# Four attention layers on one core: the order in which TensorE takes the four heads of a block of keys

## The chip, the cores and the metric

The kernel runs on one core of a Trainium2 chip. The metric is the device time of one execution in microseconds (us). Before the change three runs took 3563.54, 3566.97 and 3571.05 us; the median is 3566.97. One further execution was profiled: it took 3571.17 us, and the span from its first to its last instruction is 3569.3 us.

## The reference

Four decoder layers follow one another on x of shape (4, 512, 256), with one context ctx of the same shape; D = 256, 16 heads of 16 (the last layer: 8 heads of 32). Cut to what matters:

```python
def _L0_xattn_ref(x, context, ...):           # causal self, then cross attention, both with a length rule
    z = _mha(x, x, Wq1, Wk1, Wv1, mask0, causal=True)
    x1 = _layernorm(x + z, ln1_g, ln1_b)
    z = _mha(x1, context, Wq2, Wk2, Wv2, mask1, causal=False)
    x2 = _layernorm(x1 + z, ln2_g, ln2_b)
    z = (relu(x2 @ fc1_w.T + fc1_b) * mask0 @ fc2_w.T + fc2_b) * mask0
    return _layernorm(x2 + z, ln3_g, ln3_b)

# L1: two attentions with an integer mask each, wo, rms norms, then a mixture of 8 experts (+1 shared)
    scores = einsum('bhqd,bhkd->bhqk', q, k) / sqrt(DK)
    scores = where(mask[:, None, :, :] == 0, NEG, scores)
    attn = softmax(scores, axis=-1)
    out = einsum('bhqk,bhkd->bhqd', attn, v)     # then reshape and @ wo

# L2: two attentions with a mask, biases, wo and a layer norm, then relu(x @ w1 + b1) @ w2 + b2
# L3: one causal attention with 8 heads of 32, and a layer norm
x = L0(x, ctx); x = L1(x, ctx, mask_ik0, mask_if1); x = L2(x, ctx, mask_ik0, mask_if1); x = L3(x, ctx, ctx)
```

## The kernel before

The program runs ten stages in the order a0 a1 f0 a2 a3 moe a4 a5 f2 a6. The f and moe stages are the dense layers and have code of their own (`feed_block`). The a stages are the seven attentions: a0 is L0's causal self attention, a1 L0's cross attention, a2 and a3 are L1's two, a4 and a5 L2's two (these four have a mask), a6 is L3's. Pairs of them (a0 a1, a2 a3, a4 a5) and a6 alone are built by `attention_block`.

**Units, turns, blocks, steps.** A unit is one stage for one batch row: 16 heads, 512 queries, 512 keys. It is worked in four turns (index j, or u inside the unit) of four heads each (two heads in a6). A turn goes over four blocks of 128 keys. In a0 to a5 a block has two steps (couples = 2), each for a couple of heads; so a turn has 8 steps (halves = 8) and a unit has 16 blocks. In a6 a block has one step.

**What a step holds.** The letters in brackets are those of the list of work.

- [ST] key scores, L720: two products, keys on the partitions, of 64 rows each (a head's parts stacked; the two heads of a couple lie in partitions 0 to 63 and 64 to 127), into one of two PSUM buffers `scores`.
- [S] query scores of the turn two ahead, L753: two products of the same shape the other way round, each into one bank of a ring of three banks (RB). DVE reads each (L993 with a mask, L991 without) for the least value of each query, and so frees the bank. In the causal stages two products with the causal triangle (L759) are added.
- [exp] on TensorE the mask products, L738 (L736 the causal triangle): two products of 128 rows onto the key scores; in a1 there are none. On ScalarE the exponential of the buffer, L882, into probT.
- [PV] once a block, L774: value product of the block before (four heads, in passes of 128 rows and 32 columns), summed over the four blocks in one bank `outputs`.

The two `scores` buffers let key scores run up to two steps ahead of the exponentials; the wait is `c_exp` two steps back.

**Small and long work beside the steps.** `timetable` puts each of the other operations at a step of the unit: per turn oT (ScalarE copies `outputs`) and m (TensorE transposes the least values; ScalarE and DVE make mrow of them) at its step 1, mrows and stack (SP's transfers into Q and K) at step 2; q, k, V, mT (the mask transposed), x, c, len (a0 and a1) of the next unit, and on, ot, y, ln of the unit before (steps 2 to 7 of its first turn). All that TensorE writes in these (m, q, k, V, mT, x, c, len, on, ot, y) takes a bank of the same ring of three as S. A bank is given out in the order of the list and may be written when the third entry before has been read (`bank_free`).

**What sets the order.** `schedule` yields one list for all engines. Each engine's program walks this list and does what is its own in each entry, in order; semaphores tie them. So a change in the order of the list moves ScalarE's and DVE's work along with TensorE's. SP and POOL take only their own entries (stack, mrows, loads, norms). Before the change the list has, for every step: ST, S, exp, then the small work of that step, and at every even step the PV of the block before.

**Stacking.** `stack` (L557, L559, L565) sends 13 transfers, 15 in a0 and a1, which lay out Q and K of the turn three ahead; the first S of that turn waits for them. `minimum_rows` (L576) sends mrow into Q and is issued by SP just ahead of `stack`; it waits for m.

Of the kernel before, what the change touches and what calls it, by code (L numbers as in the profile page):

```python
# [14 lines left out]
B, S, D = 4, 512, 256  # L15
P = 128
KB = D // P
QT = S // P
# [117 lines left out]
def timetable(a):  # L136

    h, out = a.halves, []
    step = h // 4
    for qt in range(QT):  # L140
        out += [(2 + qt, "on", -1, qt), (3 + qt, "ot", -1, qt), (4 + qt, "y", -1, qt),
                (qt + (5 if a.wo else 3), "ln", -1, qt)]
    for u in range(QT):
        out += [(u * h + 1, "oT", 0, u - 1), (u * h + 1, "m", 0, u + 1),
                (u * h + step, "mrows", 0, u + 1), (u * h + step, "stack", 0, u + 3)]
    out += [(6, "len", 1, 0), (h + 6, "len", 1, 1), (6, "maskld", 1, 0), (10, "maskcv", 1, 0)]
    out += [(h + 1, "q", 1, 1), (h + 2 * step, "k", 1, 1), (2 * h + 1, "V", 1, 0), (2 * h + 2 * step, "V", 1, 1)]
    out += [(2 * h + n * step, "mT", 1, n) for n in range(QT)]
    out += [(2 * h, "cnld", 2, 0), (2 * h, "tokens", 2, 0), (2 * h + 2 * step, "norms", 2, 0),
            (2 * h + 3 * step, "kvld", 2, 0), (3 * h, "x", 2, 0), (3 * h, "x", 2, 1)]  # L150
    out += [(3 * h + step, "c", 2, 0), (3 * h + step, "c", 2, 1), (3 * h + 2 * step, "q", 2, 0),
            (3 * h + 3 * step, "k", 2, 0)]
    out += [(0, "wload", 0, 0), (1, "wscale", 0, 0), (2 * h + 3, "rawload", 0, 0)]
    return out


def wanted(work, a, st, b, first):

    n = int(st[1:])
    return {"ot": a.wo, "y": a.wo, "ln": a.ln, "len": a.length, "maskld": a.mask is not None,  # L160
            "maskcv": a.mask is not None, "mT": a.mask is not None, "cnld": a.kv == "mctx",
            "c": a.kv == "mctx", "kvld": a.kv == "ctx", "tokens": a.rms or a.length, "norms": a.rms,
            "wload": b == 1 and 1 <= n < len(ATT) - 1, "wscale": b == 2 and n < len(ATT) - 1,
            "rawload": b == 2 and first and st != "a6"}.get(work, True)


def schedule(stages, base):

    units = [(st, b) for st in stages for b in range(B)]
    end = base + len(units)  # L170
    halves = ATT[int(stages[0][1:])].halves
    couples = halves // QT
    for j in range(4 * base - 6, 4 * end + 2):
        m, u = divmod(j, 4)

        def there(g):
            return base <= g // 4 < end

        beside = {}
        for t, work, ahead, n in timetable(ATT[int(stages[0][1:])]):  # L180
            beside.setdefault(t, []).append((work, ahead, n))
        for h in range(halves):
            if there(j):
                yield ("ST", j, h)
            if there(j + 2):
                yield ("S", j + 2, h)
            if there(j):
                yield ("exp", j, h)
            for work, ahead, n in beside.get(u * halves + h, []):
                if work in ("oT", "stack", "m", "mrows"):  # L190
                    if there(4 * m + n):
                        yield (work, 4 * m + n, 0)
                    continue
                k = m + ahead
                if base <= k < end:
                    st, b = units[k - base]
                    if wanted(work, ATT[int(st[1:])], st, b, st == stages[0]):
                        yield (work, k, n)
            kb = h // couples - 1
            if h % couples == 0:  # L200
                if kb >= 0 and there(j):
                    yield ("PV", j, kb)
                if kb < 0 and there(j - 1):
                    yield ("PV", j - 1, QT - 1)

# [4 lines left out]
def build(nc, io, ctx):  # L212
# [189 lines left out]
    def attention_block(mem, stages):  # L402
# [40 lines left out]
        block = mem.enter_context(nc.Block())  # L443

        work = list(schedule(stages, base))


# [1050 lines left out]
```

How the kernel before makes its waits and increments, by code:

```python
    def wait_x(eng, st, b):  # L347
        before = ORDER[ORDER.index(st) - 1]
        if st == "a0":
            eng.wait_ge(*((c_x0, 16) if type(b) is int and b == 0 else (c_x, 16)))
        elif before == "moe":
            eng.wait_ge(c_hD.sem, c_hD.at(st, 0, 0))
        elif before[0] == "f":
            eng.wait_ge(c_xout.sem, c_xout.at(before, b, QT))
        else:
            eng.wait_ge(*x_done[before, b, QT - 1])
# [1 line left out]
    def wait_weights(eng, n):  # L359
        eng.wait_ge(c_w[n % 2], 48 * (n // 2 + 1))
# [1 line left out]
    def deviation(pool, st, b, qt, eps):  # L362
        r = qt % 2
        pool.wait_ge(c_var.sem, c_var.at(st, b, qt + 1))
        pool.tensor_tensor(ve[:, r, :], mv[:, r, 1:2], eps_of[eps], ALU.add)
        pool.drain()
        pool.tensor_tensor(rstd[:, r, :], ve[:, r, :], minus_half[:, 0:1], ALU.pow).then_inc(c_rstd.sem, 1)
# [1 line left out]
    def gain(pool, st, b, qt, gamma, beta):  # L370
        pool.wait_ge(c_xh.sem, c_xh.at(st, b, qt + 1))
        pool.tensor_tensor(xh[:, qt % 2, :], xh[:, qt % 2, :], gamma, ALU.mult)
        pool.drain()
        pool.tensor_tensor(tile(b, qt), xh[:, qt % 2, :], beta, ALU.add).then_inc(c_xout.sem, 1)
# [9 lines left out]
    def centre(dve, st, b, qt):  # L385
        r = qt % 2
        dve.wait_ge(c_rstd.sem, c_rstd.at(st, b, qt + 1))
        dve.wait_ge(c_xout.sem, c_xout.at(st, b, max(qt - 1, 0)))
        dve.tensor_scalar(xh[:, r, :], y[:, r, :], mv[:, r, 0:1], rstd[:, r, :], ALU.subtract,
                          ALU.mult).then_inc(c_xh.sem, 1)
```

## Time and profile before

| | |
|---|---|
| median of three runs | 3566.97 us (3563.54 to 3571.05) |
| the profiled execution | 3571.17 us, span 3569.3 us |
| granted TensorE clock, mean | 0.905 |
| PE busy | 3069.8 us, 86% |
| DVE busy | 1923.2 us, 54% |
| ACT busy | 1455.1 us, 41% |
| POOL busy | 451.6 us, 13% |

PE is TensorE's matmul side, PEld its weight loads, DVE VectorE, ACT ScalarE, POOL GpSimd, SP SyncE (its queue: SPq). Busy shares are means over ten unlike stages. A matmul's end is modelled, and matmuls overlap; so the distance from the start of one group to the start of the next tells more than durations do. The granted clock is 1.0 where TensorE runs at 2.4 GHz and 0.5 where it runs at 1.2 GHz.

### The profile page before, as it was taken

Reading aid. Unit: us, or ns where it says so; the run is one execution under the profiler, and the core shown is the slowest. Engines: PE = TensorE matmul, PEld = TensorE weight load, DVE = VectorE, ACT = ScalarE, POOL = GpSimd, SP = SyncE. Lnnn points to the kernel's source line nnn. Section 1 sums busy time; section 2 is a strip of 40 time slices with the busy share of each in tenths; the row PEclk is TensorE's granted clock in tenths of the full one; section 3 lists DMA queues with packets and bytes.
Section 4 is the critical chain, followed back from the end, with each engine's and each line's share of the span. In section 5 each row is a group of like instructions: output and inputs, shape, how many; then the busy total and the mean of one; then the engine's idle time right before and its main releaser. Section 6 shows DMA issues by size and latency. Waiting matters only on the chain. (4 is left out here: it accounts for less than half of the span.)

```text
span 3569.3 us, 47592 instructions
## 1 busy us (share of the span) xinstructions
PE 3069.8 (86%) x16790; PEld 1814.4 (51%) x16912; DVE 1923.2 (54%) x4573; ACT 1455.1 (41%) x2134; POOL 451.6 (13%) x538
## 2 busy tenths in 40 slices
PE   6888878855999999899999999988999999784775
PEld 3444333232344444389898989963443343373443
DVE  4555777655666666443333333335777777443333
ACT  1333444431555555444444444423555554431222
POOL 0011111033112110010000000010111122121011
PEclk7888898876999999989999999998999999887777
DMA  2112121101222222000000000002222222001221
GB/s 90 47 38 54 44 65 45 33 1 41 72 66 85 59 83 57 17 24 24 25 25 25 24 25 25 1 15 57 74 81 66 77 61 52 1 1 40 52 64 40
DMA packets 95789, 158.42 MB, mean 44 GB/s; under 512 B 28520, under 2 KB 38120, under 8 KB 93368
## 3 DMA queue, kind: packets, MB, share of 16 engines
q1 hardware_dynamic: 95544, 155.24, 15.5%
q8 instruction: 144, 2.36, 0.3%
q14 instruction: 101, 0.83, 0.1%
HBM read 60.76 MB, written 2.10 MB: 18 GB/s over the span
## 5 line engine op out<-in xcount | busy, mean ns | idle before, releaser
L882 ACT ACTIVATE probT_a<-scores 128x1024 f32<-128x1024 f32 (+3 forms) x832 | 785.2, 949 | 1004.3 <-PE scores L738 477.4
L993 DVE CUSTOM_DVE_ANT_0 ring<-ring,maskb_a 128x512 f32<-128x512 f32 x1024 | 681.8, 716 | 211.2 <-PE ring L753 208.3
L753 PE MATMUL ring<-K_a,Q_a 64*128 64x512 f32 (+7 forms) x1664 | 466.7, 437 | 161.5 <-DMA Q_a<-fixed_a 97.3
L774 PE MATMUL outputs<-probT_a,V_a 128*32 128x512 f32 (+6 forms) x3328 | 470.9, 606 | 27.1 <-ACT oT_a L889 13.2
L1325 DVE TENSOR_TENSOR hidden_moe<-whole_moe,hidden_moe 128x512 fp32r<-128x512 f32 x288 | 199.8, 694 | 530.6 <-ACT whole_moe L1247 530.4
L1168 PE MATMUL scores<-tokens_moe,weights_moe 128*128 128x512 f32 x1728 | 455.1, 400 | 10.7 <-issue 10.7
L991 DVE TENSOR_REDUCE negm_a<-ring 128x1 f32<-128x512 f32 (+3 forms) x640 | 329.8, 561 | 237.1 <-PE ring L759 181.5
L720 PE MATMUL scores<-Q_a,K_a 64*128 64x512 f32 (+7 forms) x1664 | 425.8, 489 | 3.8
L720 PEld LDWEIGHTS scores<-Q_a,K_a 64*128 64x128 f32 (+1 forms) x1664 | 171.6, 193 | 482.6 <-issue 359.8
L1181 PE MATMUL ring<-weights_moe,hidden_moe 128*128 128x256 f32 x2592 | 402.7, 283 | 2.2 <-DVE hidden_moe L1325 1.5
L753 PEld LDWEIGHTS ring<-K_a,Q_a 64*128 64x128 f32 (+1 forms) x1664 | 243.0, 204 | 278.9 <-DMA Q_a<-fixed_a 113.5
L1181 PEld LDWEIGHTS ring<-weights_moe,hidden_moe 128*128 128x128 f32 x2592 | 367.7, 191 | 28.2 <-DVE X L1305 4.1
L1247 ACT ACTIVATE hidden_moe<-scores 128x512 fp32r<-128x512 f32 x288 | 172.0, 597 | 454.0 <-PE scores L1168 452.1
L1168 PEld LDWEIGHTS scores<-tokens_moe,weights_moe 128*128 128x128 f32 x1728 | 313.6, 193 | 65.7 <-issue 12.6
L738 PE MATMUL scores<-maskT_a,identb 128*128 128x512 bf16 x902 | 286.1, 388 | 13.5 <-issue 13.3
L1034 DVE SCALAR_TENSOR_TENSOR parts_a<-ring,wcol,parts_a 128x512 fp32r<-128x512 f32 x112 | 84.1, 751 | 188.3 <-ACT parts_a L918 188.3
L829 PE MATMUL ring<-xT_a,wt 128*128 128x512 f32 x320 | 176.8, 685 | 10.0 <-DVE negm_a L993 4.0
L691 POOL TENSOR_TENSOR ve<-mv,epsilon 128x1 f32<-128x1 f32 x80 | 15.2, 189 | 1240.3 <-DVE mv L964 1240.3
L774 PEld LDWEIGHTS outputs<-probT_a,V_a 128*32 128x32 f32 (+1 forms) x3328 | 77.0, 114 | 185.9 <-ACT probT_a L882 89.9
L1247 ACT ACTIVATE whole_moe<-scores 128x512 f32<-128x512 f32 x288 | 171.1, 594 | 0.0
L685 POOL TENSOR_SCALAR maskb_a<-maski_a 128x2048 bf16<-128x2048 int32 x16 | 113.7, 7105 | 396.0 <-DMA maski_a<-in_mask 307.5
L1181 PE MATMUL outputs<-weights_moe,hidden_moe 128*128 128x256 f32 x864 | 150.9, 283 | 0.0
(152 smaller groups left out, 3114.3 us busy)
## 6 DMA issues: line engine op xcount, KB each, us to landing
Q_a<-parts_a SPq DMA_DIRECT2D x672, 64.0 KB
K_a<-parts_a SPq DMA_DIRECT2D x672, 64.0 KB
raw<-in_moew SPq DMA_DIRECT2D x9, 2048.0 KB, 7.7
maski_a<-in_mask SPq DMA_DIRECT2D x16, 1024.0 KB, 5.2
wt<-in_w SPq DMA_DIRECT2D x7, 1024.0 KB, 4.8
Q_a<-mrow_a SPq DMA_DIRECT2D x416, 4.0 KB
kvT_a<-in_ctxT SPq DMA_DIRECT2D x12, 512.0 KB, 3.5
wrow<-in_row SPq DMA_DIRECT2D x7, 512.0 KB, 5.5
```

The lines of the kernel that those rows point to most:

```text
L720: last = pe.matmul(scores_bank(j, h)[:, e, q0:S], K[rows, g, kb * P:(kb + 1) * P], Q[rows, g, q0:S], start=True, stop=not (a.causal or a.m ...
L738: last = pe.matmul(out, identb[:, :], maskT[:, m % 2, kb, :], start=False, stop=True)
L753: last = pe.matmul(bank("S", j, n, e)[:, 0:w], Q[rows, g, qt * P:(qt + 1) * P], K[rows, g, 0:w], start=True, stop=not a.causal)
L774: last = pe.matmul(OB[x * slot:(x + 1) * slot, q0:S], V[:, m % 2, kb, c:c + slot], probT[:, kb % 2, x, q0:S], start=(kb == 0), stop=(kb == ...
L829: last = pe.matmul(out[:, :], wt[:, k, kb, c0:c0 + P], src[:, kb, :], start=(kb == 0), stop=(kb == KB - 1))
L882: act.activation(probT[:, kb % 2, 2 * p:2 * p + 2, q0:S], scores_bank(j, n)[:, :, q0:S], ACT.Exp, bias=0.0, scale=-1.0).then_inc(c_exp.sem, 1)
L991: least = dve.tensor_reduce(out, sc, AX.X, ALU.min)
L993: least = dve.tensor_tensor_reduce(sc, sc, maskb[:, m % 2, qt, :], 1.0, BIG * 2, ALU.add, ALU.min, out)
L1168: last = pe.matmul(bank, w1(slot, a, kb, n), tokens[:, c, kb, unit * S:(unit + 1) * S], start=(kb == 0 and (a, c) == PARTS[0]), stop=(kb = ...
L1181: last = pe.matmul(OUTS[t][:, 0:D], hidden[:, i % 4, a, t * P:(t + 1) * P], w2(slot, c, n), start=(n == 0 and (a, c) == PARTS[0]), stop=(n ...
L1247: last = act.activation(dst, RING[m % 4], ACT.Silu)
L1325: dve.tensor_tensor(hidden[:, m % 4, 1, :], whole[:, m % 2, :], hidden[:, m % 4, 0, :].bitcast(F32), ALU.subtract).then_inc(c_low.sem, 1)
```

## The change

In `schedule` the loop over steps becomes a loop over the blocks of keys. The small work moves into a local function `aside(h)`, the same as before but for the name "split" in a tuple, which nothing yields.

```diff
-        for h in range(halves):
-            if there(j):
-                yield ("ST", j, h)
-            if there(j + 2):
-                yield ("S", j + 2, h)
-            if there(j):
-                yield ("exp", j, h)
+        def aside(h):
             for work, ahead, n in beside.get(u * halves + h, []):
-                if work in ("oT", "stack", "m", "mrows"):
+                if work in ("oT", "stack", "split", "m", "mrows"):
...
-            kb = h // couples - 1
-            if h % couples == 0:
-                if kb >= 0 and there(j):
-                    yield ("PV", j, kb)
-                if kb < 0 and there(j - 1):
-                    yield ("PV", j - 1, QT - 1)
+
+        for kb in range(QT):
+            steps = range(kb * couples, (kb + 1) * couples)
+            for h in steps:
+                if there(j):
+                    yield ("ST", j, h)
+            if there(j + 2):
+                yield ("S", j + 2, steps[0])
+            for h in steps:
+                if there(j):
+                    yield ("exp", j, h)
+            if couples == 1:
+                yield from aside(kb)
+            if kb and there(j):
+                yield ("PV", j, kb - 1)
+            if not kb and there(j - 1):
+                yield ("PV", j - 1, QT - 1)
+            if couples > 1:
+                if there(j + 2):
+                    yield ("S", j + 2, steps[1])
+                for h in steps:
+                    yield from aside(h)
```

So a block of two steps was: ST(0) S(0) exp(0) small(0) PV, ST(1) S(1) exp(1) small(1). It becomes: ST(0) ST(1) S(0) exp(0) exp(1) PV S(1) small(0) small(1). All buffers, banks, semaphores and waits stay; the ring's order of banks follows the list. For couples = 1 (a6) the list is the same as before.

## Rows read from the trace of the kernel before

**Rows 1.** The page, busy time, share of the span and instructions of each engine.
```profile
PE 3069.8 (86%) x16790; PEld 1814.4 (51%) x16912; DVE 1923.2 (54%) x4573; ACT 1455.1 (41%) x2134; POOL 451.6 (13%) x538
```

**Rows 2.** Stretches: us, busy PE, PEld, DVE, ACT, POOL, clock, DMA; about a0, a1, a3, a4.
```profile
28.00:390.00 362.00, 302.34 (x1757) 151.82 (x1757) 205.45 (x473) 114.57 (x184) 31.72 (x52) 0.80 0.18 47
390.00:745.00 355.00, 275.59 (x1358) 106.37 (x1355) 237.40 (x460) 158.22 (x197) 45.57 (x79) 0.86 0.16 41
...
1170.00:1515.00 345.00, 323.26 (x1765) 134.19 (x1796) 214.13 (x603) 186.67 (x238) 35.67 (x14) 0.99 0.20 55
2400.00:2740.00 340.00, 311.44 (x1542) 131.13 (x1569) 234.72 (x657) 157.17 (x199) 63.60 (x55) 0.94 0.25 69
```

**Rows 3.** Timeline of PE in a2: start, busy us, engine, line, tiles, shape, count.
```profile
1117.13 0.40 PE L753 MATMUL ring<-K_a,Q_a 64*128 64x512 f32 x2
1117.47 0.61 PE L738 MATMUL scores<-maskT_a,identb 128*128 128x512 bf16 x2
1118.00 0.51 PE L720 MATMUL scores<-Q_a,K_a 64*128 64x512 f32 x2
1118.34 0.54 PE L753 MATMUL ring<-K_a,Q_a 64*128 64x512 f32 x2
1118.81 0.61 PE L738 MATMUL scores<-maskT_a,identb 128*128 128x512 bf16 x2
1119.25 1.88 PE L829 MATMUL ring<-kvT_a,wt 128*128 128x512 f32 x4
1121.06 1.06 PE L774 MATMUL outputs<-probT_a,V_a 128*32 128x512 f32 x8
1122.06 0.50 PE L720 MATMUL scores<-Q_a,K_a 64*128 64x512 f32 x2
```

**Rows 4.** Timeline of all engines in a2, around one transpose m.
```profile
1107.69 0.40 PE L753 MATMUL ring<-K_a,Q_a 64*128 64x512 f32 x2
...
1108.12 0.70 DVE L993 CUSTOM_DVE_ANT_0 ring<-ring,maskb_a 128x512 f32<-128x512 f32 x1 [0.90 <-PE ring L753]
...
1108.46 0.27 PE L799 MATMUL ring<-identf,negm_a 128*32 128x128 f32 x1
...
1108.66 1.02 ACT L882 ACTIVATE probT_a<-scores 128x1024 f32<-128x1024 f32 x1 [1.52 <-PE scores L738]
...
1109.58 0.18 PEld L753 LDWEIGHTS ring<-K_a,Q_a 64*128 64x128 f32 x1 [0.47 <-DVE negm_a L993]
...
1110.65 1.81 SPq L576 DMA_DIRECT2D Q_a<-mrow_a  x2
```

**Rows 5.** PE's waits: two for a2 to a5, two for a0 and a1.
```profile
PE ring L753 <- DMA Q_a<-fixed_a: 33.5, 14, 8.2
...
PE ring L753 <- DVE negm_a L993: 6.6, 32, 0.4
...
PE ring L753 <- DMA K_a<-pen_a: 23.5, 13, 5.4
PE ring L753 <- DVE negm_a L991: 19.6, 41, 1.4
```

**Rows 6.** Timeline of PE in a1.
```profile
557.64 0.40 PE L753 MATMUL ring<-K_a,Q_a 64*128 64x512 f32 x2
557.87 0.39 PE L720 MATMUL scores<-Q_a,K_a 64*128 64x512 f32 x2
...
558.82 0.50 PE L753 MATMUL ring<-K_a,Q_a 64*128 64x512 f32 x1 [0.32 <-DVE negm_a L991]
```

**Rows 7.** Timeline of PE in a2, the mask's transposes ahead of a value product.
```profile
1179.67 0.39 PE L842 MATMUL ring<-identb,maskb_a 128*128 128x128 bf16 x4
1179.99 1.07 PE L774 MATMUL outputs<-probT_a,V_a 128*32 128x512 f32 x8
```

**Rows 8.** Timeline of DVE in a3, the first output's division.
```profile
1208.84 0.24 DVE L1050 RECIPROCAL rinv_a<-ring 128x16 f32<-128x16 f32 x1
1209.15 0.42 DVE L1058 TENSOR_TENSOR o_a<-ring,rinv_a 128x256 f32<-128x256 f32 x1
```

## The prediction

> **What bounds the kernel now.** I read the page's busy line first: PE holds 86% of the span, DVE 54%, ACT 41% [rows 1]. That is a mean over unlike stages, so the next view is the table of stretches [rows 2]. The diff acts in a0 to a5; a6 has one head pair a block, and with couples = 1 the new loop yields the old order word for word. The reader is to see two kinds of stage. In a2 to a5 (masked, 1373 us in all) PE is busy for 92 to 94% at a granted clock of 0.93 to 0.99. In a0 and a1 (717 us) it is busy for 78 to 84% at 0.80 to 0.86: something else holds it there.
>
> The third view is PE's timeline. I call the two key score products of a step ST, its two query score products S, its mask products P, the eight passes of the value product PV, and give each group the time from its start to the next group's. In a masked stage [rows 3]: S 0.34 when a P follows, P pair 0.53 when ST follows, ST 0.34, S 0.47, P pair 0.44 when k follows, k 1.81, PV 1.00. All of it is back to back: PE's order is the path.
>
> The fourth view is all engines around one small transpose [rows 4]. S issued at 1107.69; DVE took its first bank at 1108.12, 0.43 later, and works on one for 0.70. The second matmul of the next S, whose weights load at 1109.58, came 1.89 after the S before it: three ring banks, two held by S, one by the transpose m, so it has to wait until DVE has read both. With nothing between, only the first must be read: in rows 3 the S at 1118.34 is two matmuls of 0.50 merged to 0.54, so the second began at 1118.38, **1.25** after 1117.13, and P followed 0.43 later. These two distances, **1.25** (no small work between two S) and **1.89** (one piece between), are DVE's and do not depend on PE's order.
>
> The fifth view is the list of waits [rows 5]: a2 to a5 lose 33.5 us to the transfers that stack Q and K (much of it at each block's start), a0 and a1 23.5 to the same transfers (their last writes K from pen) and 19.6 to DVE.
>
> **The change part by part.** No instruction is added or removed, no DMA either; everything is order. Every engine walks the same list: on ACT exp(1) now stands ahead of the small work of step 0, on DVE the reading of S(1) does; SP and POOL skip the moved entries, and what they do themselves (stack, mrows, loads, norms) keeps its order there. A block (128 keys, four heads) goes from ST S P · ST S P · PV with small work after either P, to ST ST S P P · PV · S · small work.
>
> *Mode changes.* A P pair costs 0.53 before ST and 0.44 before a product of its own shape [rows 3]. In a1 an S that follows ST, ST, S without a break costs 0.23 (557.64 to 557.87) [rows 6] against 0.34 for the first pair after another shape (1118.00 to 1118.34) [rows 3]. A block without small work goes from five changes to three: I reckon 3.54 before (0.53+1.00+0.34+0.33+0.53+0.34+0.47) and, if nothing waited, 0.96 (four P) + 1.00 + 0.34 + 0.23 + 0.23 + 0.33 = 3.09 after. With small work the count stays at five: S(1) becomes a lone pair after PV (0.44 instead of 0.33), the second ST falls from 0.34 to 0.23. Nothing is won there.
>
> *What waits instead.* Before, PV and a P pair lay between the two S of a block, and P and ST between S(1) and the next S. Now all P and PV lie on one side (S(0) to S(1): 0.33+0.96+1.00 = 2.29), and from S(1) to the next S(0) only small work and two ST: 0.80 bare. DVE's 1.25 or 1.89 ends last there. From the first P of a block to that of the next, in a masked stage (16 blocks a unit):
> - no small work (3 blocks): 3.54 before; after 0.96+1.00+1.25+0.43 = 3.64. +0.10 each, +0.3. exp is close too: 1.02 each, the first starting 0.64 after its P (1108.66 less 1107.69 + 0.33) [rows 4], so the second is done at 2.6 and the second ST wants it at 2.5; DVE's 1.25 covers that.
> - mT alone (2): before 0.44+0.32+1.00+0.34+0.33+0.53+0.34+0.47 = 3.77 [rows 3, 7]; after 0.96+1.00+1.89+0.43 = 4.28. +0.51, +1.0 for both. Before, mT sat on the side that had PV as cover.
> - m alone (1): before 0.53+1.00+0.34+1.89+0.43 = 4.19, after 4.28: +0.1.
> - m then q (1), mT then m then V (1): the second piece needs the bank of S(1)'s first result (1.25), the third that of its second (1.89). Before they were spread over both steps. +0.3 and +0.7.
> - the end of the last unit (3 blocks: on, ot, y four times each): ot needs DVE's o. Now on(0) stands behind both results of S(1) on DVE, which have been read at 1.7; the product starts 0.31 behind its reciprocal and takes 0.42 [rows 8], so ot can start 2.5 after S(1) where PE is there at 1.0, and on(1) and the next ST are queued behind it. With the rows of PE between (on 0.59, ot 0.25) the block grows from 5.32 to 6.20: +0.9. The next two wait for a bank (1.89), for o and for ACT's copy of ot, +0.5 to 0.6 each: +2.0 a unit in a2, a3. In a4, a5 y brings four DVE operations instead of one; the third block before already waited for them, so I take +1.5.
> - long work (k, q, k, V: 4) covers DVE: -0.06 each; x, x, m gains 0.2: -0.45.
>
> Sum a unit +4.0 (a2, a3) and +3.5 (a4, a5); with 8 units each +32 + 28 = **+60 us**. Bounds: nothing waits (three blocks a unit win 0.45, 16 units: -22, call it -15 with exp) and twice the second and third items (+80).
>
> *The stack transfers.* SP sends mrow and then the stack of the turn three ahead; S(0) of the next turn waits. mrow is made behind exp(1) and oT on ACT, so SP starts 2.19 after m (1110.65 less 1108.46) [rows 4], 4.83 after the turn's first P (0.53+1.00+0.34+0.33+0.44+2.19). Now exp(1) follows exp(0) at once, since its P does: exps done at 2.6, oT some 0.5, mrow's two copies 0.25 and 0.28: 4.0. SP starts 0.8 earlier, while S(0) stands 0.23 later behind a second ST. In a2 to a5 the steady waits are small (0.3 us in half of 64 turns) and go, those at the two blocks' starts shrink by 0.8 a turn: **-10**, between 0 and -20.
>
> *a0.* Causal P and the causal part of S alternate with row pairs in both orders, so mode changes stay at five. Three of four turns wait at S(0) for the stack. Their length is that chain; the same sum with a0's narrower products makes it 0.45 shorter in two (estimate), 1.9 in the turn with x, whose exp(1) had stood behind x and PV. 2.8 by four units: **-11**, between 0 and -20.
>
> *a1.* No P. Before, two S stood 0.46 apart after the odd step, so its second matmul waited for DVE (557.64 to 558.82, 1.18) [rows 6] and PV queued behind it. Now PV covers one of the two distances: 1.00+1.25+0.43 = 2.68 instead of 2.94 bare, 4.25 instead of 5.02 with k or q. Per unit some 4 us of PE, of which the stack chain takes back all but its own shortening and one turn: I keep 3.5 by four, **-14**, between 0 and -25.
>
> Sum: 60 - 10 - 11 - 14 = **+25 us** on the profiled execution's 3571.2. The median of the runs is 4.2 lower: 3567.0 + 25 = **3592 us**.
>
> A rule speaks for the other side. The Trainium skill, "TensorEngine Tiling (Array Packing)", Key Properties, says that changing the tiling mode, not merely the tile, drains TensorE. The trace agrees: 0.53 against 0.44 for the same P pair. By the rule alone the time would come out as in rival 1 below; it says nothing of who waits for DVE.
>
> **The rivals.**
> 1. *Faster, the mode changes decide.* For it: 0.53 against 0.44, 0.34 against 0.23, PE at 94%. If DVE's two distances don't end later than PE's own work: -15 in a2 to a5, with -10 -11 -14 from the rest: -50, 3517; half of the waits appearing, about 3545. Against it: the 1.25 is already reached in nearly every bare pair of steps.
> 2. *No change.* The chain of stack transfers sets the turns. Where a turn grows less than its wait for the stack, the growth is hidden. For: S(0) waits for it in about half of the masked turns. Against: 33.5 us in all, much of it at the starts [rows 5], can't hide 60, and the growth lies in the turns with on/ot/y and with V, the longest. It gives 3567, from 3560 to 3574.
> 3. *Slower by more, through DVE's queue and the clock.* In a4, a5 the norm's operations run into the next turn; PE's pauses near 2 us there make the clock fall to its 1.2 GHz level, at which a0, with a mean of 0.80, spends some 40% of its time [rows 2]. Taken as twice the time, 3.5% of 1373 us at it adds some 50: 3640. It decides once pauses come in every turn.
>
> **How the numbers follow.** My forecast (3575 to 3620) 0.45; rival 1 0.27; rival 2 0.12; rival 3 0.16. The likeliest gives 3592. For 8 in 10 I reach to the half-waits of rival 1 and to the lower part of rival 3: 3532 to 3632. Within 0.2% (7 us, what a measurement tells from no change) 0.11; faster 0.29; slower 0.60.
>
> **What would show it.** Right: in a2 to a5 S(1) followed by a late second matmul of the next S(0), 1.25 or 1.89 after it, 4.28 us blocks where mT stands alone, ot waiting for o by more than 1 us, "PE ring L753 <- DVE negm" growing from 6.6 us to tens; S bare after S(1) 0.23. Waits for the stack shrinking in all stages, a0 and a1 each shorter by 10 to 15. Wrong: a2 to a5 shorter than before, or the growth sitting on exp or on a lower granted clock.

## The result, and the profile after

The changed kernel takes **3639.7 us** (median of 4 runs, 3637.8 to 3653.4) against 3569.0 for the kernel before (4 runs, 3563.5 to 3573.5): 1.021 times as long, interval 1.018 to 1.024. Slower, as forecast, but by 71 us and not by 25, and outside the range given. The profiled execution took 3637.8, its span is 3636.0. In the file after, every line used here stands 10 further down than before: S L763, ST L730, P L748, PV L784, exp L892, DVE's score reading L1003 (masked) and L1001.

The page after, busy line and the group of S's weight loads (busy, mean ns | idle before, and what ended it):

```profile
PE 3091.1 (85%) x16804; PEld 1828.5 (50%) x16912; DVE 1924.1 (53%) x4573; ACT 1433.0 (39%) x2134; POOL 452.4 (12%) x538
...
L763 PEld LDWEIGHTS ring<-K_a,Q_a 64*128 64x128 f32 (+1 forms) x1664 | 233.4, 200 | 627.7 <-DVE negm_a L1003 205.3
```

Every engine is busy for about as long as before, in a longer span [rows 1]. So nothing was added; something waits, and the second row points at it: the weight load of a score product that waits for DVE's reading of a ring bank. Next, stretches of the two traces that hold the same work (a0 and a1, a2 and a3, a4 and a5, each a little inside its ends; columns as in rows 2). After:

```profile
60.00:756.00 696.00, 554.45 (x3102) 259.81 (x3102) 439.19 (x916) 270.69 (x388) 81.11 (x136) 0.84 0.17 43
836.00:1548.00 712.00, 643.44 (x3289) 267.59 (x3342) 429.92 (x1208) 337.55 (x441) 92.06 (x37) 0.96 0.21 58
2445.00:3182.00 737.00, 657.99 (x3330) 279.72 (x3385) 481.73 (x1348) 337.04 (x440) 123.69 (x139) 0.96 0.20 56
```

Before:

```profile
60.00:763.00 703.00, 562.54 (x3104) 253.83 (x3104) 439.11 (x918) 276.81 (x388) 80.89 (x136) 0.83 0.17 43
840.00:1519.00 679.00, 630.19 (x3288) 264.10 (x3348) 433.26 (x1210) 346.89 (x443) 94.80 (x37) 0.96 0.22 61
2425.00:3117.00 692.00, 635.83 (x3300) 270.59 (x3362) 476.68 (x1339) 343.78 (x439) 123.39 (x139) 0.96 0.21 58
```

The granted clock is the same in all three pairs within 0.01. Measured between the dense stages (lines as before: a0 and a1 up to f0's first L1181 product; the others from the last L1181 product of the dense stage ahead to the next one's first L1215 product in a2, a3 and first L1181 product in a4, a5), a0 and a1 went from 763.3 to 756.5 (-6.7), a2 to a5 from 1450.6 to 1524.3 (**+73.7**), everything else by -0.1: +66.7 in all. How far such a figure of one execution can be trusted is seen from runs whose order in a0 and a1 is the same: with the changed order there, this run has 756.5, e6 below 763.3 and e8 757.7; with the old one, 763.3 and 763.9. So +73.7 is clear, and -6.7 lies between 0 and -7.

**A block without small work.** All engines after, in a2:

```profile
1160.33 1.04 PE L748 MATMUL scores<-maskT_a,identb 128*128 128x512 bf16 x4
...
1160.97 1.94 ACT L892 ACTIVATE probT_a<-scores 128x1024 f32<-128x1024 f32 x2 [0.74 <-PE scores L748]
...
1161.30 1.06 PE L784 MATMUL outputs<-probT_a,V_a 128*32 128x512 f32 x8
...
1162.30 0.50 PE L763 MATMUL ring<-K_a,Q_a 64*128 64x512 f32 x2
...
1162.64 0.83 PE L730 MATMUL scores<-Q_a,K_a 64*128 64x512 f32 x4
1162.83 0.70 DVE L1003 CUSTOM_DVE_ANT_0 ring<-ring,maskb_a 128x512 f32<-128x512 f32 x1 [0.51 <-PE ring L763]
...
1163.30 0.84 PE L763 MATMUL ring<-K_a,Q_a 64*128 64x512 f32 x2
1163.45 0.73 DVE L1003 CUSTOM_DVE_ANT_0 ring<-ring,maskb_a 128x512 f32<-128x512 f32 x1
1163.64 0.18 PEld L763 LDWEIGHTS ring<-K_a,Q_a 64*128 64x128 f32 x1 [0.38 <-DVE negm_a L1003]
...
1164.08 0.82 PE L748 MATMUL scores<-maskT_a,identb 128*128 128x512 bf16 x3
```

Follow S(1) at 1162.30. DVE starts on its first bank at 1162.83 and on the second at 1163.45; only then is the first bank free, and the weights of the second matmul of the next S(0) load at 1163.64, 1.34 after S(1). P follows at 1164.08, so the block is 3.75 long where 3.64 was forecast. The S(0) at 1163.30 is two matmuls (0.39 and 0.50) that with the wait between them stretch to 0.84.

**A block with mT.** PE's timeline after:

```profile
1181.76 0.50 PE L763 MATMUL ring<-K_a,Q_a 64*128 64x512 f32 x2
1182.19 0.40 PE L852 MATMUL ring<-identb,maskb_a 128*128 128x128 bf16 x4
1182.52 0.73 PE L730 MATMUL scores<-Q_a,K_a 64*128 64x512 f32 x4
1183.11 0.49 PE L763 MATMUL ring<-K_a,Q_a 64*128 64x512 f32 x1
1183.75 0.50 PE L763 MATMUL ring<-K_a,Q_a 64*128 64x512 f32 x1 [0.16 <-DVE negm_a L1003]
1184.19 1.04 PE L748 MATMUL scores<-maskT_a,identb 128*128 128x512 bf16 x4
1185.15 1.06 PE L784 MATMUL outputs<-probT_a,V_a 128*32 128x512 f32 x8
```

The second matmul of S(0) comes 1.99 after S(1) (forecast 1.89). Here the wait, 0.16, stands in a row of its own; the block, 1180.76 to 1185.15 by its PV, takes 4.39. Four P take 0.96 (1184.19 to 1185.15), as the prediction has it: the saving by mode changes exists.

**The waits after**, from a2 to a5 (total us, times, longest):

```profile
PEld ring L763 <- DVE negm_a L1003: 205.3, 321, 1.6
...
PE ring L868 <- DVE o_a L1068: 30.9, 24, 1.6
...
PE ring L763 <- DMA Q_a<-fixed_a: 24.9, 6, 8.2
...
PE ring L763 <- DVE negm_a L1003: 13.5, 38, 1.3
```

PE's own wait for DVE only doubled, 6.6 to 13.5 [rows 5]. The weight loads ahead of the matmuls show more. Before they had:

```profile
PEld ring L753 <- DVE negm_a L993: 33.5, 71, 0.8
```

That is 33.5 us in 71 waits before and 205.3 in 321 after. Such a sum is a sign and not the time lost, since a weight load may wait while the matmuls before it still run: e1 below has 181.7 us in 333 of these waits, none over 0.8, and takes 69 us less. The distances from group to group measure the loss. ot's wait for o is 1.3 us on average, as forecast; the stack's waits fell from 33.5 to 24.9.

**A fall of the clock.** In a4 and a5 one block shows more than a wait. PE's timeline after, and the stretch behind it with the columns of rows 2:

```profile
2671.93 0.50 PE L763 MATMUL ring<-K_a,Q_a 64*128 64x512 f32 x1
2673.44 0.50 PE L763 MATMUL ring<-K_a,Q_a 64*128 64x512 f32 x1 [1.02 <-DVE negm_a L1003]
...
2674.74 2.76 PE L839 MATMUL ring<-xT_a,wt 128*128 128x512 f32 x4 [0.36 <-DVE negm_a L1003]
```

```profile
2675.00:2680.00 5.00, 5.00 (x14) 1.61 (x13) 2.44 (x8) 0.95 (x2) 4.09 (x3) 0.66 0.04 9
```

PE waits 1.02 and 0.36 us for DVE within 3 us, and then the granted clock is 0.66 in these five: part of them is run at 1.2 GHz. The block takes 9.13 us. It comes seven times in a4 and a5; at 2930.8 it does the same (9.19), the others take 6.12 to 7.86. That is 3 us in all.

### The profile page after: what moved, and what is told of

It reads as the page before. It is cut to its first block and busy times, and to the rows that moved or that the text cites. A ratio compares the mean times of both kernels' runs of the same rounds, so it can differ in the third digit from the quotient of the medians.

```text
span 3636.0 us, 47606 instructions
## 1 busy us (share of the span) xinstructions
PE 3091.1 (85%) x16804; PEld 1828.5 (50%) x16912; DVE 1924.1 (53%) x4573; ACT 1433.0 (39%) x2134; POOL 452.4 (12%) x538
## 5 line engine op out<-in xcount | busy, mean ns | idle before, releaser
L892 ACT ACTIVATE probT_a<-scores 128x1024 f32<-128x1024 f32 (+3 forms) x832 | 748.4, 948 | 810.2 <-PE scores L748 382.1
L1003 DVE CUSTOM_DVE_ANT_0 ring<-ring,maskb_a 128x512 f32<-128x512 f32 x1024 | 684.7, 717 | 298.6 <-PE ring L763 296.0
L763 PE MATMUL ring<-K_a,Q_a 64*128 64x512 f32 (+7 forms) x1664 | 515.4, 471 | 199.9 <-DMA Q_a<-fixed_a 91.3
L763 PEld LDWEIGHTS ring<-K_a,Q_a 64*128 64x128 f32 (+1 forms) x1664 | 233.4, 200 | 627.7 <-DVE negm_a L1003 205.3
L784 PE MATMUL outputs<-probT_a,V_a 128*32 128x512 f32 (+6 forms) x3328 | 458.3, 591 | 13.2 <-ACT oT_a L899 7.3
L1001 DVE TENSOR_REDUCE negm_a<-ring 128x1 f32<-128x512 f32 (+3 forms) x640 | 330.7, 563 | 237.3 <-PE ring L769 191.6
L730 PE MATMUL scores<-Q_a,K_a 64*128 64x512 f32 (+7 forms) x1664 | 339.0, 447 | 5.3 <-ACT probT_a L892 5.0
L748 PE MATMUL scores<-maskT_a,identb 128*128 128x512 bf16 x916 | 243.0, 383 | 17.0 <-issue 16.9
L730 PEld LDWEIGHTS scores<-Q_a,K_a 64*128 64x128 f32 (+1 forms) x1664 | 150.6, 195 | 203.2 <-issue 134.7
L928 ACT ACTIVATE parts_a<-ring,wcol 128x512 fp32r<-128x512 f32 x112 | 77.1, 688 | 261.4 <-PE ring L839 261.4
L784 PEld LDWEIGHTS outputs<-probT_a,V_a 128*32 128x32 f32 (+1 forms) x3328 | 76.0, 113 | 172.0 <-issue 144.0
```

The source lines that it names most:

```text
L730: last = pe.matmul(scores_bank(j, h)[:, e, q0:S], K[rows, g, kb * P:(kb + 1) * P], Q[rows, g, q0:S], start=True, stop=not (a.causal or a.m ...
L748: last = pe.matmul(out, identb[:, :], maskT[:, m % 2, kb, :], start=False, stop=True)
L763: last = pe.matmul(bank("S", j, n, e)[:, 0:w], Q[rows, g, qt * P:(qt + 1) * P], K[rows, g, 0:w], start=True, stop=not a.causal)
L784: last = pe.matmul(OB[x * slot:(x + 1) * slot, q0:S], V[:, m % 2, kb, c:c + slot], probT[:, kb % 2, x, q0:S], start=(kb == 0), stop=(kb == ...
L892: act.activation(probT[:, kb % 2, 2 * p:2 * p + 2, q0:S], scores_bank(j, n)[:, :, q0:S], ACT.Exp, bias=0.0, scale=-1.0).then_inc(c_exp.sem, 1)
L1001: least = dve.tensor_reduce(out, sc, AX.X, ALU.min)
```

## The experiments

Each is compared with the kernel before on the same chip. All edits but e7's are made to the changed kernel. A block is ST ST S(0) P P PV S(1), then small work.

**e1: half of the small work ahead of PV.**

```
-    if couples == 1: yield from aside(kb)
+    yield from aside(steps[0])        # then PV, S(1)
-    for h in steps: yield from aside(h)
+    yield from aside(steps[1])
```

> The changed kernel with one entry moved: the small work of a block's first step stands ahead of PV again (ST ST S P P small(0) PV S small(1)), that of the second step stays after S(1). Theory A (DVE's reading of the ring of three banks ends last between S(1) and the next S(0); small work put there takes a bank and makes 1.35 us into 1.99): blocks with mT alone fall from 4.39 to about 3.95, on/ot/on from 6.33 to about 4.9, y/ot/on and y/ot/y by 0.7 each, mT/m/V by 0.4; k, q lose 0.25 in four blocks. About 3 us a unit in a2 to a5, 16 units: 3638 - 49 = 3590; with a0 and a1, where DVE then has S between on and ln and no longer waits 1.00 us for POOL twice a unit, another -16: 3575. Theory B (grouping the four heads costs by itself: the second ST waits for the second exponential, P and P hold it back): nothing moved here touches it, 3625 to 3640.

Measured: 3571.1 (10 runs), ratio 1.001 [0.999, 1.003], 69 us below the changed kernel. a2 to a5 take 1476.1 (+25 on before), a0 and a1 738.4 (-25). So the place of one half of the small work relative to PV, with all P and ST grouped as in the change, is worth nearly the whole loss. That alone doesn't yet say through which resource.

**e2: S(1) ahead of PV as well.**

```
+    if couples > 1 and there(j + 2): yield ("S", j + 2, steps[1])
     ... PV ...
-    if there(j + 2): yield ("S", j + 2, steps[1])
```

> The changed kernel with S(1) ahead of PV (ST ST S P P S PV small(0) small(1)): one more change of shape in blocks without small work, but PV now covers DVE between S(1) and the next S(0), and four P cover it between S(0) and S(1) (0.33 + 0.96 = 1.29 against DVE's 1.25). Theory A: blocks without small work 3.30 (3.74 in the changed kernel, 3.54 before), mT alone about 3.6 (4.39), m alone 3.5 (4.39); turns come down to the chain of the stack's transfers, about 17.8 us; a2 to a5 some 9 us a unit below the changed kernel less the transfers' floor, about 8; all in all 3535, from 3515 to 3560. Theory B: the second exponential still ends at 2.6 after the first P and the grouped heads stay, 3600 or more.

Measured: 3615.8, ratio 1.014 [1.010, 1.018]: missed by 80. In a2 to a5 the bare block does what was expected. PE's timeline of e2:

```profile
1152.72 1.06 PE L784 MATMUL outputs<-probT_a,V_a 128*32 128x512 f32 x8
1153.71 0.75 PE L730 MATMUL scores<-Q_a,K_a 64*128 64x512 f32 x4
1154.30 0.40 PE L763 MATMUL ring<-K_a,Q_a 64*128 64x512 f32 x2
1154.63 1.04 PE L748 MATMUL scores<-maskT_a,identb 128*128 128x512 bf16 x4
1155.60 0.50 PE L763 MATMUL ring<-K_a,Q_a 64*128 64x512 f32 x2
1156.03 1.07 PE L784 MATMUL outputs<-probT_a,V_a 128*32 128x512 f32 x8
```

From PV to PV it is 3.31, against 3.74 in the changed kernel (median) and 3.54 before: with P between the two S on one side and PV on the other, no S holds PE up in this block, and the mode change saved (four a block instead of five) shows. But a0 and a1 grew to 805.3 (+42). There no P (or a causal one only) stands between S(0) and S(1), so in a1 they are adjacent, four banks are wanted of three, and PV queues behind the wait. e2's waits in a0 and a1:

```profile
PE ring L763 <- DVE negm_a L1001: 48.5, 61, 2.2
PE ring L763 <- DVE o_a L1068: 45.7, 14, 3.5
```

The first was 19.6 before [rows 5]. The expectation had priced a2 to a5's pattern only. In a4 and a5 (749.3, +13 on before) the blocks with on and y also grew; that DVE has the norm's operations and both S to read in a row there is how I read it, and no run tests it.

**e3: S(1) and the first half of the small work ahead of PV.** e1's and e2's edits together, in the order small work, S(1), PV.

> Both: ST ST S P P small(0) S PV small(1). Theory A: like the run before, but on(0) is read by DVE ahead of S(1) and so ot no longer waits for o (a unit's three blocks of on, ot, y gain some 1.5), and DVE has S between on and ln in a0, a1 (no wait for POOL, -16 in all); against that the second S waits up to 0.3 where one small piece of work holds a bank between the two S. Some 10 to 20 below the run before: 3520. Theory B: 3600 or more.

Measured: 3545.7 (10 runs), ratio 0.994 [0.993, 0.996]: faster than before, by 23 and not by 48. a2 to a5 take 15 less than before, a0 and a1 15 less. One thing left out in the sum is another engine's reading. PE's timeline of e3 (a block with x; the lines stand 8 further down than before):

```profile
1164.21 1.04 PE L746 MATMUL scores<-maskT_a,identb 128*128 128x512 bf16 x4
1165.08 1.04 PE L818 MATMUL ring<-identf,xs_a 128*128 128x128 f32 x8
1166.05 0.50 PE L761 MATMUL ring<-K_a,Q_a 64*128 64x512 f32 x1
1167.42 0.49 PE L761 MATMUL ring<-K_a,Q_a 64*128 64x512 f32 x1 [0.87 <-ACT xT_a L911]
```

x fills two banks that ACT empties; S right behind waits 0.87 for it, and PV behind S. In a2 to a5 there are 12 such waits, 9.9 us of the 25 missing; the rest wasn't taken apart.

**e4: ln one step later**, the changed order otherwise.

```
-    (qt + (5 if a.wo else 3), "ln", -1, qt)
+    (qt + (5 if a.wo else 4 if a.length else 3), "ln", -1, qt)
```

It tests a row of the trace after that the prediction had no word for. DVE in a1, after:

```profile
506.78 0.18 DVE L974 BATCH_NORM_AGGREGATE mv<-bn 128x2 f32<-128x6 f32 x1
507.96 0.41 DVE L1088 TENSOR_SCALAR xh<-y,mv,rstd 128x256 f32<-128x256 f32 x1 [1.00 <-POOL rstd L703]
508.29 0.25 DVE L1060 RECIPROCAL rinv_a<-ring 128x16 f32<-128x16 f32 x1
```

POOL turns the aggregated variance into rstd; DVE, which works in order, stands for 1.00 us before the centring, and everything queued behind it, the readings of S too. Before, both readings of S lay between the aggregate and the centring, and this wait is rare in a0 and a1 (5 times, 4.4 us).

> The changed kernel with ln one step later in a0 and a1 alone (timetable 4 instead of 3), so that DVE reads S between on and ln. Theory C (a0 and a1 miss the gain forecast because DVE, in order, waits 1.00 us for POOL's rstd right behind bn_aggr, twice a unit; before, the two results of S stood between): -2.0 a unit, 8 units: a0 and a1 shorter by 16, 3640 - 16 = 3624, and DVE xh<-y waits of 1.00 gone. Rival (the turn with len is bound by DVE's work or by len's own round trip, the wait for POOL only takes its place): within 3 of 3640.

Measured: 3623.2, ratio 1.016 [1.012, 1.020], 16 us below the changed kernel, as expected of the theory that holds POOL's answer to be the cause. The same wait over a0 and a1, after:

```profile
DVE xh L1088 <- POOL rstd L703: 18.0, 18, 1.0
```

and in e4:

```profile
DVE xh L1088 <- POOL rstd L703: 5.1, 2, 2.6
```

a0 and a1 fell from 756.5 to 743.5 (by 13 to 20 against the three executions that have the changed order there); a2 to a5, whose code is the same, are 6 longer, and all the rest is 5 shorter.

**e5: an order for each kind of stage.**

```
+    early = couples == 1 or not masked or u != 2
+    if early: yield from aside(steps[0])
+    if masked and there(j + 2): yield ("S", j + 2, steps[1])
     ... PV ...
+    if not masked and there(j + 2): yield ("S", j + 2, steps[1])
+    if not early: yield from aside(steps[0])
+    yield from aside(steps[1])
```

> The best of the orders by stage, as the blocks of the three runs before show it: a0, a1 with small(0) ahead of PV and S(1) behind it (738 us to the end of a1 against 748 and 763); a2 to a5 with small(0) and S(1) ahead of PV, but in the third turn of a unit (mT, V) both pieces of small work behind PV. Theory A: against the run with both moved (3546), a0 and a1 give 10, and the third turn falls from 21.0 to 19.2 us, 1.8 by 16 units = 29: 3507, from 3495 to 3525. Rival (the turns are bound by the stack's transfers at some 18 us, a shorter turn gives the time back as a wait of S(0) in the next): 3530.

Measured: **3524.1** (5 runs, 3516.6 to 3525.2), ratio 0.986 [0.984, 0.988], the fastest of all. a2 to a5 are 25 below before, a0 and a1 18. It is 17 above the sum made for it. Counted from PV to PV, the third turn of a unit (mT, V) takes 20.7 in a2 and a3 (19.2 expected, 21.0 in e3), the second 17.7 (18.4 in e3), the others 17.7 and 20.9 as in e3: 1.0 a unit less instead of 1.8, which leaves out some 13 us. And a0 and a1, expected at 738, took 745.0 in the very order in which e1 took 738.4; that gain was the scatter of one execution. The rival's floor, the stack's transfers, is not what the trace shows: PE waits for them 6 times in a2 to a5 (29.5 us), in 64 turns.

**e6 and e7: DVE reads half as much**, in the changed kernel (e6) and in the kernel before (e7). In a2 to a5 it reads 256 of each bank's 512 columns, and exp's scale is set so that the values stay small.

```
-    w = a.width(qt)
+    w = a.width(qt) if a.mask is None else S // 2
-    bias=0.0, scale=-1.0
+    bias=0.0, scale=-1.0 if a.mask is None else -1e-6
```

> The changed kernel where DVE reads 256 of the 512 columns of each S result in a2 to a5 (half of the row minimum is left out, and exp is scaled so that it stays finite; instructions, semaphores and order stay). DVE's 0.65 a result becomes about 0.38. Theory A: the two distances fall from 1.35 and 1.99 to 1.08 and 1.45, blocks without small work from 3.74 to about 3.47, with mT or m alone from 4.39 to about 3.85, the unit from 83.5 to about 79: 3640 - 75 = 3565. Theory B (the second exponential): blocks without small work stay at 3.7, 3620 or more.

> The kernel before with the same half reading. Theory A: it loses only its own small waits (0.1 a bare pair, 0.6 at m), 1.5 to 2.5 a unit: 3545; so the difference to the changed kernel with half reading is 25 or less, where it is 71 with full reading. Theory B: the difference stays at 60 or more.

Measured: e6 3555.3, ratio 0.996 [0.994, 0.997]; e7 3537.6, ratio 0.991 [0.989, 0.993]; 10 and 7 below what was expected. The reading's mean fell from 717 to 449 ns (e6). The difference between the orders fell from 71 us to **18**, in a2 to a5 alone from 74 to 22 (1435.5 against 1413.3). The same mode changes, exps and transfers are in both; only DVE's reading became shorter. So some 50 of the 74 us go with DVE's readings. A part of this fall is the stack's: in a2 to a5 PE's waits for its transfers grew in e7 from 33.5 us in 14 waits to 50.3 in 32, in e6 only from 24.9 to 31.8. Taken off on both sides, the difference falls from 82 to 41. So it is 40 to 50 of the 74 that are DVE's readings ending last. e6's page, and its waits in a2 to a5:

```profile
L1003 DVE CUSTOM_DVE_ANT_0 ring<-ring,maskb_a 128x256 f32<-128x256 f32 x1024 | 415.8, 449 | 437.4 <-PE ring L763 428.9
```

```profile
PEld ring L763 <- DVE negm_a L1003: 70.8, 120, 1.1
```

It was 205.3 in 321 waits in the changed kernel. PE's timeline of e6, the same kind of block as the first one shown:

```profile
1103.37 1.04 PE L748 MATMUL scores<-maskT_a,identb 128*128 128x512 bf16 x4
1104.34 1.07 PE L784 MATMUL outputs<-probT_a,V_a 128*32 128x512 f32 x8
1105.34 0.50 PE L763 MATMUL ring<-K_a,Q_a 64*128 64x512 f32 x2
1105.67 0.83 PE L730 MATMUL scores<-Q_a,K_a 64*128 64x512 f32 x4
1106.34 0.57 PE L763 MATMUL ring<-K_a,Q_a 64*128 64x512 f32 x2
1106.85 1.04 PE L748 MATMUL scores<-maskT_a,identb 128*128 128x512 bf16 x4
```

3.48 instead of 3.75; S(0) to P is 0.51 where it was 0.78. It is still not the 3.09 of a block in which nothing waits: four ST take 0.67 (0.59 in e2 at 1153.71) and S(0) is still held a little.

**e8: a shorter exp, DVE as it was.** exp covers 512 of 1024 columns in a2 to a5 (the unread probabilities are set to 1 once).

> The changed kernel where ScalarE takes the exponential of 256 of the 512 queries in a2 to a5 (the other half of probT holds ones): 1.02 becomes about 0.6. Theory A: DVE's distances end last anyway, 3635, from 3625 to 3645. Theory B (the second ST of a block waits for the second exponential): 3590 or less.

Measured: 3644.6, ratio 1.021 [1.018, 1.023], no gain, with exp at 595 ns instead of 1022 in 560 of its calls. The block without small work is 3.74 as in the changed kernel, and so are all the others within 0.02, but for m and q in a4 and a5. The weight loads of ST waited for exp 37.4 us in 84 waits (a2 to a5, changed kernel) and now 8.4 in 10, and nothing is gained by it. The rival by which the second exp holds ST, and so the block, falls. The block of m and q there takes 8.9 to 9.5 four times of seven here and twice in the changed kernel, which adds 5 us.

## Why the direction was right and the size wrong

**The mechanism held.** Putting both P pairs and PV on one side of S(1) leaves DVE's distance as what ends last on the other. Median block lengths, in a2 and a3 where nothing else is said, us. Before they are counted from the first P pair of a block to that of the next, as the prediction counts them, afterwards from PV to PV. Where the prediction gives no length, a star marks the trace's median before, and that with the prediction's growth added:

```
small work in the block     before  forecast  measured   e6 (half read)
none                         3.54     3.64      3.74        3.47
mT                           3.77     4.28      4.39        3.86
m                            4.19     4.28      4.39        3.86
m, q                         5.69*    5.99*     6.12        5.85
m, q (a4, a5)                6.50*    6.80*     7.65        6.52
mT, m, V                     5.92*    6.62*     6.78        6.25
on, ot, on                   5.32     6.20      6.33        5.80
twice y, ot, on              6.30*    6.85*     7.23        6.89
twice y, ot, on (a4, a5)     6.31*    6.86*     7.92        7.72
y, ot, y                     5.34*    5.89*     6.25        6.24
y, ot, y (a4, a5)            6.65*    6.65*     6.68        6.24
```

**Step that failed first: the distances 1.25 and 1.89,** said not to depend on PE's order. They were read where S follows a product of its own tile shape. In the new order S(1) always follows PV, whose shape is another. DVE starts 0.53 after it (1162.30 to 1162.83) where it was 0.43 [rows 4], and the distances become 1.35 and 1.99. In a2 to a5 this is regular: where DVE stood idle it started a median 0.43 after the pair in 232 pairs behind ST before, and 0.54 in 224 behind PV after; the distance with nothing between the S is 1.24 in most of 152 places before and 1.35 in 76 after. Some 12 blocks in 16 end on one of them: 0.10 x 12 x 16 units = 19 us. The prediction had this row's cost on PE's side (0.34 against 0.23 for a first pair) and left it out on DVE's.

**Second: +1.5 a unit for on, ot and y in a4 and a5, and +0.3 for m and q.** The block that has y, ot, on twice takes 7.92 there where 6.86 comes out of the prediction, and m and q, the first of the next turn, 7.65 instead of 6.80: 1.9 a unit too little, 15 us (a small part of it is the longer distance again). "The third block before already waited for them" was true, and that block did not grow (6.65 to 6.68); it didn't bound the one ahead of it and the one behind it. That it is the four DVE operations which y brings that delay the readings of S there is argued from the list of work; e6 gives m and q back whole (6.52), the block with y, ot, on twice by 0.2 only. In a2 and a3 the two blocks with y are 0.4 above the forecast each, and y, ot, y stays at 6.24 with half the reading, so something other than DVE's reading sets it; what, stays open. e2's and e3's expectations, built on a2's blocks, failed in part at the same place.

Turn by turn (medians) a unit of a2 and a3 grew by 5.8 and one of a4 and a5 by 6.5, against 4.0 and 3.5 forecast: +98 where the sum said +60. The stages grew by 74. Of the -24 between, 8.6 are the prediction's -10 for the stack transfers: PE's waits for them fell from 33.5 to 24.9, and from 14 times to 6. (That S(0) waits for them in half of the turns before was misread; the trace has 14 waits in 64 turns.) The other 15 lie at the starts and ends of the blocks of units and weren't taken apart. So the blocks were missed by 38 and the stages by only 24 (74 against 60 - 10); the 15 between is luck.

**Third: a0 and a1, -25 forecast, -6.7 measured** (0 to -7, as said above). The sums took in PE, exp and the stack chain. They had DVE only as a reader of S. In the new order its list puts the centring directly behind the aggregate, with POOL's answer still due: 18 waits of 1.00 where there were 5, on an engine that works in order. e4 takes nearly all of them away and gets 13 of the 18 missing us back in a0 and a1; e1, which has the 5 of before, has the full -25 in the one execution profiled, and e5, with the same order there, -18. That the waits for the stack would shrink here was wrong: 23.5 us before [rows 5], 27.3 after.

**The mode changes.** Four P in a row take 0.96 where two and two took 0.53 each, and the first pair of S after another shape takes 0.34 against 0.23. The Trainium skill's "TensorEngine Tiling (Array Packing)", Key Properties, says that a change of mode drains TensorE. The trace agrees that a change costs time, some 0.1 us each. For the change's own order the saving is 0.45 a block at most, and DVE's wait took all of it; e2's bare block, with one mode change fewer than before and the P together, gets 0.23 (3.54 to 3.31).

**The rivals.** Rival 1 (faster) was wrong as priced for this order, and right about what was to be had: e5, in which the S are spread over the block again and the P and ST stay together, gains 44. Rival 2 has a small part: growth that takes the place of waits for the stack, 8.6 us. Rival 3 gave 3640, nearly the measured time, and that is luck too. Its first half, blocks growing in a4 and a5 behind the norm's operations, is seen; its second, the clock falling after PE's pauses, is seen twice, for 3 us and not for 50: the mean clock stayed at 0.96 as before in the same stretches.

Not settled: how much of the remaining 22 us between e6 and e7 is still reading (449 ns instead of 717 is not zero) and how much the waits of ot for o, 23.2 us in 25 waits in e6.

## What to carry to other kernels

When products that fill a small ring of banks are regrouped, lay out the fill times and ask of each fill when its reader will have emptied the bank it needs: evenly spread fills are worth more than saved mode changes, and both can be had (e5). Move the work that covers the reader (PV, P) between the fills, never to one side of them. Walk every engine's own list in the new order, not only that of the bound engine: DVE's one-microsecond stand for POOL in a1 came from two entries becoming neighbours. Read a distance only from a place with the same predecessor as in the new order. And before a stage's time from one execution goes into a sum, look how far it moves where nothing in it was changed: 7 us here.

## What the runs showed of the hardware

- A product's reader starts later when the product is the first after a change of tile shape: DVE began 0.53 us after the start of such a score pair (behind PV in the changed kernel), 0.43 after one without a change (behind ST before); behind P, another shape again, it was 0.53 in e2 (median of 17). The pair itself holds PE for 0.34 instead of 0.23.
- Halving what DVE reads of a bank (512 to 256 columns) took the operation from 717 to 449 ns, and the bank's release also waits for a read of the accumulator of 141 ns. Halving exp from 1024 to 512 columns took it from 1022 to 595 ns. Both have a fixed part, by an estimate from the two sizes some 180 and 170 ns.
- The round trip from DVE's aggregate over POOL's rstd back to DVE left DVE idle for 1.00 us, the same in nearly all of its 18 occurrences (18.0 in all).
- In the changed kernel PE waited 1.02 and 0.36 us for DVE within 3 us, and the granted clock was 0.66 in the 5 us from 2675.00 on; the q product that began there took 2.76 us, where the k product of the same shape takes 1.88 in rows 3. Two of seven such blocks had it.
